# Attention on one core: the maxima transposed once per block, and the softmax sums inverted on GpSimd

## What is computed

```
xn = group_norm(x, gn_gamma, gn_beta)
qkv = einsum('bchw,oc->bohw', xn, w_qkv).reshape(B, 3, nh, d, H * W)   # nh = 4, d = 64, H * W = 4096
q, k, v = qkv[:, 0], qkv[:, 1], qkv[:, 2]
scores = einsum('bhci,bhcj->bhij', q, k) * d ** (-0.5)
attn = softmax(scores, axis=-1)
out = einsum('bhij,bhcj->bhci', attn, v).reshape(B, C, H, W)
return xn + einsum('bchw,oc->bohw', out, w_proj) + b_proj
```

## Time and profile before

| | before |
|---|---|
| time, median of 3 runs | 5567.9 us (5565.55 to 5569.24) |
| span of the profiled execution, first to last instruction | 5568.2 us |
| TensorE busy | 5050.2 us (91%) |
| VectorE busy | 4172.1 us (75%) |
| GpSimd busy | 3191.6 us (57%) |
| ScalarE busy | 2291.1 us (41%) |
| transposes of the maxima (L801) | 128 |
| reciprocals (L1816) | 256, 135.9 us |

### The profile page before, as it was taken

The page is one execution under the profiler, slowest core; times in us unless marked ns, Lnnn a source line. Parts: engine busy times, 40 slices in busy tenths (PEclk is TensorE's granted clock), DMA queues, the critical chain, the costliest instruction groups (busy, mean ns, idle before and its releaser), DMA issues. The chain is left out here.

```text
span 5568.2 us, 75691 instructions
## 1 busy us (share of the span) xinstructions
PE 5050.2 (91%) x23148; PEld 2344.5 (42%) x23148; DVE 4172.1 (75%) x6834; ACT 2291.1 (41%) x4176; POOL 3191.6 (57%) x2819
## 2 busy tenths in 40 slices
PE   7999999999799999999978869969997996999688
PEld 3333333333333333333336657645543553555344
DVE  4888888885488888888633334448986896888898
ACT  2444444443244444444401112125544554555455
POOL 0666666656056666666617757746555663665675
PEclk9999999999899999999978879979998998999899
DMA  2000000000100000000034435559987998999999
GB/s 72 1 1 1 1 1 1 1 1 2 61 1 1 1 1 1 1 1 1 1 92 124 127 103 159 162 205 374 370 332 296 383 377 309 375 388 359 381 410 359
DMA packets 320281, 812.36 MB, mean 146 GB/s; under 512 B 70094, under 2 KB 137556, under 8 KB 319758
## 3 DMA queue, kind: packets, MB, share of 16 engines
q0 software_dynamic: 193536, 679.59, 32.4%
q1 hardware_dynamic: 126478, 129.39, 6.8%
HBM read 708.40 MB, written 100.43 MB: 145 GB/s over the span
## 5 line engine op out<-in xcount | busy, mean ns | idle before, releaser
L638 POOL TENSOR_TENSOR arena<-arena 128x512 f32<-128x512 f32 x960 | 1406.1, 1465 | 828.9 <-ACT arena L1265 764.4
L1265 ACT ACTIVATE arena<-ps 128x1024 f32<-128x1024 f32 x1024 | 1049.6, 1025 | 1239.4 <-PE ps L816 1209.9
L1788 DVE TENSOR_REDUCE arena<-ps 128x2 f32<-128x1024 f32 x1024 | 1243.1, 1214 | 347.3 <-PE ps L790 347.2
L690 POOL DMA_INDIRECT arena<-corners,arena x1152 | 1092.4, 948 | 694.5 <-issue 303.1
L2018 DVE SCALAR_TENSOR_TENSOR ps<-arena,ps 128x256 f32<-128x256 f32 x2304 | 955.8, 483 | 235.6 <-DVEq L2012 226.4
L1139 PE MATMUL ps<-arena 128*128 128x512 f32 x2304 | 1050.4, 599 | 0.2
L816 PE MATMUL ps<-arena 64*128 64x512 f32 x4096 | 1046.0, 589 | 0.0
L829 PE MATMUL ps<-arena 128*64 128x512 f32 x4096 | 991.3, 605 | 0.0
L1810 DVE TENSOR_TENSOR arena<-arena 128x512 f32<-128x512 f32 x960 | 888.6, 926 | 62.5 <-ACT arena L1265 62.1
L674 POOL DMA_INDIRECT arena<-corners,arena x576 | 545.0, 946 | 275.1 <-issue 243.9
L1450 ACT ACTIVATE ps<-arena 128x256 f32<-128x256 f32 x1152 | 499.2, 469 | 453.3 <-DMA arena<-corners,arena 198.7
(11 more groups left out here) (161 smaller groups left out, 3777.0 us busy)
## 6 DMA issues: line engine op xcount, KB each, us to landing
corners<-arena SPq DMA_DIRECT2D x256, 256.0 KB
arena<-corners,arena POOLq DMA_INDIRECT x1728, 9.0
img<-in_x SPq DMA_DIRECT2D x8, 1024.0 KB, 9.3
corners<-arena SPq DMA_DIRECT2D x128, 64.0 KB, 2.2
arena<-in_wd SPq DMA_DIRECT2D x2, 2304.0 KB, 8.9
between<-img SPq DMA_DIRECT2D x4, 1024.0 KB, 6.3
arena<-between SPq DMA_DIRECT2D x4, 1024.0 KB, 10.0
resid<-img SPq DMA_DIRECT2D x8, 512.0 KB
```

What stands on the lines that cost most here:

```text
L638: pool.tensor_tensor(SUMS[u % 2][:, 0, :], SUMS[u % 2][:, 0, :], P[n % 4][:, 0, :], ALU.add).then_inc(sum_a, 1)
L690: pool.indirect_dma_start(G3[4 * k + t].rearrange("p a c -> p (a c)"), None, table256[b], bass.IndirectOffsetOnAxis(ap=IS3[:, k, t:t + 1], ...
L1265: af(P[n % 4].rearrange("p h q -> p (h q)"), ps[:, 2 * (n % 2):2 * (n % 2) + 2, :].rearrange("p h q -> p (h q)"), ACT.Exp, scale=float(D) ...
L1788: v.tensor_reduce(mxp[i % 2][:, :, j], ps[:, 4:6, :], AX.X, ALU.max).then_inc(mx_done, 1)
```

## The change

The maxima of all 512 queries of a block are collected in `mxp` first, reduced once into columns 0 to 3 and 64 to 67 of `MSTAT`, and transposed once. Rows 0 to 3 of each head then hold the four quarters. ScalarE copies them four times into `MROW`, each time with a scale per partition (`OWN`), a column of a small tile that is nonzero only in the row of that quarter, so that every other row becomes zero; `COEF` has four rows of 64 for each head, and the product picks the sum of the four. The transpose stands at g % 16 == 14.

The sums are no longer inverted by VectorE. GpSimd raises them to the power -1 in four pieces of 128 columns, with a tile of -1 (`MINUS`) as the second operand: one behind the add of each of the steps 10 to 13 of the next block, and four in a row for the last block of an image.

The core of the diff (the counts in `sem_inc` and in assertions follow from it):

```diff
+        MINUS = att.f32(128)
-        mxp = [att.f32(2, QB) for _ in range(2)]
+        mxp = [att.f32(2, 4, QB) for _ in range(2)]
+        OWN = att.f32(4)
...
-            if i >= 9 and i % 8 == 1:
-                opening.append(("rows", (i - 9) // 8))
+            if i == 33:
+                opening.append(("rows", 0))
...
         def rows_in(g):
-            return (2 * g + LEAD - 1) // 8 if g % 4 == 2 and (2 * g + LEAD - 1) // 8 < 4 * BLOCKS else None
+            return (2 * g + LEAD - 1) // NT if g % (NT // 2) == NT // 2 - 2 and g + 2 < STEPS // 2 else None
...
-                    pool.memset(COEF[64 * h:64 * h + 1, :], ROW_COEF).then_inc(pool_step, 1)
+                    pool.memset(COEF[64 * h:64 * h + 4, :], ROW_COEF).then_inc(pool_step, 1)
...
+                def inverse_sums(u, i):
+
+                    pool.wait_ge(aux_done, aux_at[("sums", u)] + 1)
+                    pool.tensor_tensor(RC[:, i * 128:(i + 1) * 128], RC[:, i * 128:(i + 1) * 128], MINUS,
+                                       ALU.pow).then_inc(rc_done, 1)
...
+                pool.tensor_tensor(OWN, ident_s[:, 0:4], ident_s[:, D:D + 4], ALU.add).then_inc(pool_step, 1)
...
+                pool.tensor_scalar(OWN, OWN, 1.0 / (HALF_SCALE ** 2 * ROW_COEF), None, ALU.mult).then_inc(pool_step, 1)
...
                     if kc == 8 and u + 2 < BLOCKS:
                         cast_queries(u + 2)
+                    if 10 <= kc < 14 and u >= 1:
+                        inverse_sums(u - 1, kc - 10)
                     if kc == 16 and u >= 1:
                         normalized(u - 1)
+                for i in range(4):
+                    inverse_sums(BLOCKS - 1, i)
                 normalized(BLOCKS - 1)
...
-                        pe.wait_ge(aux_done, aux_at[("rows", 4 * u + 3)] + 1)
+                        pe.wait_ge(aux_done, aux_at[("rows", u)] + 1)
...
-                def row_copy(i):
-
-                    act.wait_ge(aux_ready, aux_at[("rows", i)] + 1)
-                    af(MROW[i // 4 % 2][:, i % 4 * 128:(i % 4 + 1) * 128], ps[:, 7, 0:128], ACT.Copy,
-                       scale=1.0 / (HALF_SCALE ** 2 * ROW_COEF)).then_inc(aux_done, 1)
+                def row_copy(u):
+
+                    act.wait_ge(aux_ready, aux_at[("rows", u)] + 1)
+                    for t in range(4):
+                        last = af(MROW[u % 2][:, t * 128:(t + 1) * 128], ps[:, 7, 0:128], ACT.Identity,
+                                  scale=OWN[:, t:t + 1])
+                    last.then_inc(aux_done, 1)
...
-                    v.tensor_reduce(mxp[i % 2][:, :, j], ps[:, 4:6, :], AX.X, ALU.max).then_inc(mx_done, 1)
-                    if j < 7:
+                    v.tensor_reduce(mxp[u % 2][:, :, t, j], ps[:, 4:6, :], AX.X, ALU.max).then_inc(mx_done, 1)
+                    if m % NT < NT - 1:
                         return
...
-                    v.tensor_reduce(MSTAT.rearrange("p (h a) -> p h a", h=2)[:, :, 0], mxp[i % 2], AX.X, ALU.max,
+                    v.tensor_reduce(MSTAT.rearrange("p (h a) -> p h a", h=2)[:, :, 0:4], mxp[u % 2], AX.X, ALU.max,
                                     negate=True).then_inc(mstat_ready, 1)
...
-                def inverse_sums(u, i):
-
-                    dve.wait_ge(aux_done, aux_at[("sums", u)] + 1)
-                    v.reciprocal(RC[:, i * 64:(i + 1) * 64], RC[:, i * 64:(i + 1) * 64]).then_inc(rc_done, 1)
...
-                    if g >= NT // 2 and 3 <= g % (NT // 2) <= 6:
-                        inverse_sums(g // (NT // 2) - 1, 2 * (g % (NT // 2) - 3))
                     add_b(2 * g)
-                    if g >= NT // 2 and 3 <= g % (NT // 2) <= 6:
-                        inverse_sums(g // (NT // 2) - 1, 2 * (g % (NT // 2) - 3) + 1)
                 add_b(STEPS - 1)
-                for i in range(8):
-                    inverse_sums(BLOCKS - 1, i)
```

More of the change, by code:

```diff
@@ L97, in program @@
         minus_half = sb("minus_half", [128, CH])
-        ARENA = 39900
+        ARENA = 39940
         arena = sb("arena", [128, ARENA])
@@ L293, in program @@
                 opening.append(("max", i))
-            if i >= 9 and i % 8 == 1:
-                opening.append(("rows", (i - 9) // 8))
-        assert ("rows", 3) in opening
+            if i == 33:
+                opening.append(("rows", 0))
+        assert ("rows", 0) in opening
         def rows_in(g):
-            return (2 * g + LEAD - 1) // 8 if g % 4 == 2 and (2 * g + LEAD - 1) // 8 < 4 * BLOCKS else None
+            return (2 * g + LEAD - 1) // NT if g % (NT // 2) == NT // 2 - 2 and g + 2 < STEPS // 2 else None
         def sums_in(g):
@@ L311, in program @@
         aux_at = {what: k for k, what in enumerate(aux)}
-        assert len(aux) == 5 * BLOCKS
+        assert len(aux) == 2 * BLOCKS
         block = ctx.enter_context(nc.Block())
@@ L426, in _ @@
                 sp.sem_inc(mx_done, -STEPS)
-                sp.sem_inc(mstat_ready, -4 * BLOCKS)
+                sp.sem_inc(mstat_ready, -BLOCKS)
                 sp.sem_inc(aux_ready, -len(aux))
@@ L436, in _ @@
                 sp.sem_inc(at_done, -BLOCKS)
-                sp.sem_inc(rc_done, -8 * BLOCKS)
+                sp.sem_inc(rc_done, -4 * BLOCKS)
                 go()
@@ L594, in _ @@
                 inverse_root(grs[:, :])
-                for what, value in ((COEF, 0.0), (MSTAT, 0.0), (ONES, 1.0)):
+                for what, value in ((COEF, 0.0), (MSTAT, 0.0), (ONES, 1.0), (MINUS, -1.0)):
                     pool.memset(what, value).then_inc(pool_step, 1)
-                pool.wait_ge(pool_step, 3)
-                pool.sem_inc(pool_step, -3)
+                pool.wait_ge(pool_step, 4)
+                pool.sem_inc(pool_step, -4)
                 for h in range(2):
-                    pool.memset(COEF[64 * h:64 * h + 1, :], ROW_COEF).then_inc(pool_step, 1)
+                    pool.memset(COEF[64 * h:64 * h + 4, :], ROW_COEF).then_inc(pool_step, 1)
                 pool.wait_ge(pool_step, 2)
@@ L617, in cast_queries @@
                                        HALF_SCALE, None, ALU.mult).then_inc(query_cast, 1)
+                def inverse_sums(u, i):
+                    pool.wait_ge(aux_done, aux_at[("sums", u)] + 1)
+                    pool.tensor_tensor(RC[:, i * 128:(i + 1) * 128], RC[:, i * 128:(i + 1) * 128], MINUS,
+                                       ALU.pow).then_inc(rc_done, 1)
                 def normalized(u):
-                    pool.wait_ge(rc_done, 8 * (u + 1))
+                    pool.wait_ge(rc_done, 4 * (u + 1))
                     pool.wait_ge(o_done, u + 1)
@@ L624, in normalized @@
                                        ALU.mult).then_inc(at_done, 1)
+                pool.tensor_tensor(OWN, ident_s[:, 0:4], ident_s[:, D:D + 4], ALU.add).then_inc(pool_step, 1)
+                pool.wait_ge(pool_step, 1)
+                pool.sem_inc(pool_step, -1)
+                pool.tensor_scalar(OWN, OWN, 1.0 / (HALF_SCALE ** 2 * ROW_COEF), None, ALU.mult).then_inc(pool_step, 1)
+                pool.wait_ge(pool_step, 1)
+                pool.sem_inc(pool_step, -1)
                 cast_queries(0)
@@ L1782, in maximum @@
                 def maximum(m):
-                    j, i = m % 8, m // 8
-                    if j == 0 and i >= 2:
-                        dve.wait_ge(mstat_ready, i - 1)
+                    u, t, j = m // NT, m // 8 % 4, m % 8
+                    if m % NT == 0 and u >= 2:
+                        dve.wait_ge(mstat_ready, u - 1)
                     dve.wait_ge(mx_ready, m + 1)
-                    v.tensor_reduce(mxp[i % 2][:, :, j], ps[:, 4:6, :], AX.X, ALU.max).then_inc(mx_done, 1)
-                    if j < 7:
+                    v.tensor_reduce(mxp[u % 2][:, :, t, j], ps[:, 4:6, :], AX.X, ALU.max).then_inc(mx_done, 1)
+                    if m % NT < NT - 1:
                         return
                     dve.wait_ge(mx_done, m + 1)
-                    if i >= 1:
-                        dve.wait_ge(aux_ready, aux_at[("rows", i - 1)] + 1)
-                    v.tensor_reduce(MSTAT.rearrange("p (h a) -> p h a", h=2)[:, :, 0], mxp[i % 2], AX.X, ALU.max,
+                    if u >= 1:
+                        dve.wait_ge(aux_ready, aux_at[("rows", u - 1)] + 1)
+                    v.tensor_reduce(MSTAT.rearrange("p (h a) -> p h a", h=2)[:, :, 0:4], mxp[u % 2], AX.X, ALU.max,
                                     negate=True).then_inc(mstat_ready, 1)
```

## The result

The changed kernel takes 7789.4 us (median of 4 runs, 7783.2 to 7796.1) against 5566.7 before: a ratio of 1.399, 95% interval 1.398 to 1.401. It is slower by 2223 us. 7600 was forecast, in a range of 5700 to 7850.

The account below looks back on a forecast made before the run. TensorE was taken to set the attention loop's pace. From the profiled 5568.2 us, minus 90 gained, plus 2022 lost in bursts and 99 at image ends, came 7599, say 7600 us; range 5700 to 7850.

Parts of the forecast that it names:

- What bounds the kernel: In the attention loop TensorE, busy 294.24 of 300 us, sets the pace; only taking work or waiting from it helps.
- The power, 19.6 us: GpSimd's power of 128 columns: 0.56 + 127 x 0.15 = 19.6 us, by a line through one and two columns.
- both doubts: On the power's line: 64 partitions against 128 with one shape against the other; long instructions may overlap their columns.
- B: Rival on GpSimd's power: columns overlap in part, 27 to 100 ns each; 6380 us at 75 ns; chance 0.20.
- C: Rival: the power runs near GpSimd's other two-input pace, 0.9 to 3.3 us; 5478 us in all; chance 0.15.
- The wait on four buffers: Step n's exponential waits for step n - 4's add; TensorE loses 4c - 13.0 us per burst, 65.4 at c = 19.6.
- The clock: After TensorE's long waits, coming back to full clock costs 0 to 2.8 us; 2 taken per burst.
- The end of an image: Four bare powers delay the projection's last chunk: 47.5 us plus 2 for the clock, twice, 99 us lost.
- The gain of 90 us: Fewer transposes (1.2 us) and no VectorE reciprocals (2.0 us): 3.2 us in each of 28 blocks.
- the third round: Round from 321.16 with reciprocals and a transpose, 1.06 us extra: 0.46 for the transpose, 0.60 for TensorE's wait.
- The masked copies, hidden: ScalarE's four copies after the one transpose, 0.27 to 0.36 us each, cost nothing, covered by 2.46 us idle.

Follow-up runs that it names:

- the four sizes: The changed kernel with powers of 8, 32, 64 and 128 columns in place of four of 128: 6368.7 us (a single run).

## Why the prediction was right, point by point

**What bounds the kernel:** right. TensorE's waits decide, and the product in place of the power shows that without them the loop is TensorE's alone.

**The power, 19.6 us:** the step that carried everything, a line through one and two columns drawn out to 128. Measured are 20.9, with 0.16 and not 0.15 us per column. That two tiny powers, one of them on 64 partitions only, came within 6% of the slope was not to be known ahead; the prediction named both doubts, and only the four sizes settle them. This term alone accounts for most of the 189 us by which 7600 was short: 4 x 1.3 us in 30 bursts are 156, and 10 more at the two ends. The rivals B and C are excluded by the four sizes: the line is straight.

The Trainium skill's rule (the page "GPSIMD Engine Reference", section "Engine selection") of about twice VectorE's time would have made an estimated 2.1 us of it. The measurement decides against it for the power: 20.9 us against 2 x 0.536 for VectorE's reciprocals of as many columns, twenty times. The product of 128 columns, 0.45 us where no add of VectorE runs at its start, is the kind of work that the page speaks of; no run has VectorE's time for it.

**The wait on four buffers:** right. The exponential of step 18 came 91.5 us after that of step 10, 91.0 by the sum, and the loss per block is 147.6 - 74.1 (the block with the product, 302.22 to 376.31 in that trace) = 73.5 us, against 4 x 20.9 - 13.0 + 2.3 = 72.9.

**The clock:** 2 us per burst were taken from between 0 and 2.8; 2.3 were measured, and 2.75 at the end of the image (6.45 - 3.70).

**The end of an image:** 47.5 us of bare waiting became 52.4. The four powers there took 83.0 us, where the prediction had 78.4.

**The gain of 90 us:** right in sum (85), wrong in its parts. The copies gained 22 us and not 34, the reciprocals' going 63 and not 56. The step that failed is "of the 1.06 of the third round what is left after 0.46 for its transpose, 0.60": that transpose cost nothing, as VectorE held up the round whether it was there or not.

**The masked copies, hidden:** right. They take 0.373 us each, a little over the 0.36 worked out, and TensorE waits for none of them (it is busy for all of the 300 us with the product).

Summed with the measured terms: 5568.2 - 85 + 30 x 73.5 + 2 x (52.4 + 2.75) = 7798, 10 us above the span. Most of the 10 is the one block that the 73.5 were read from: over the first image the bursts are 147.3 us apart on average, not 147.6.

## What to carry to other kernels

Before work is moved to an engine that looks half idle, multiply its price on that engine by its count and hold it against the idle time per block (here 84 us against 29): buffers and placing can stretch a burst, but not that sum. A price seen only at one and two elements could here be drawn out to a length; since the loop hung on that engine's queue, the slope decided and not the fixed part, so a run with a few sizes is worth its time. If the aim is to free an engine of short waits, look first for the gaps that it has: eleven reciprocals in gaps of 0.54 us cost at most 0.28 us per block on VectorE.

## What the runs showed of the hardware that was not expected

A power on GpSimd costs 0.16 us for each column from 8 to 128 columns, and 0.4 us besides: 1.65, 5.44, 10.55 and 20.79 us where no add of VectorE runs at its start. That is some sixty-four times the 0.0025 us that a column of an add of 512 takes on average (1.27 us).

A product or a power on GpSimd takes about half a microsecond longer when an add of VectorE is running as it starts: 0.90 to 0.97 instead of 0.45 for a product of 128 columns, 2.09 to 2.18 instead of 1.65 for a power of 8, 21.2 to 21.3 instead of 20.8 for one of 128. Behind the start of a power the two leave each other alone: the adds of VectorE that begin 0.3 us or more behind it and end within it take their usual 0.68 to 0.69 us, 208 of them in the trace of the changed kernel. That the two go together is shown by every instance; what they contend for is not.
